# Degree stage of a graph network kernel: a group's tile counts as one product with a 0/1 row selector, turned by way of DRAM, and five slots for the one-hots

## The reference

```python
edge_index = jnp.stack([src, dst])
x = _layernorm(x + _L0_gnn_ref(x, edge_index, edge_weight, W, b))
x = _layernorm(x + _L1_gnn_ref(x, edge_index, edge_weight1, ...))

def _L0_gnn_ref(x, edge_index, edge_weight, W, b):
    row = jnp.concatenate([edge_index[0], loop])
    col = jnp.concatenate([edge_index[1], loop])
    w = jnp.concatenate([edge_weight, jnp.ones((N,))])
    deg = segment_sum(w, row)
    dinv = where(deg > 0, safe ** -0.5, 0)
    norm_w = dinv[row] * w * dinv[col]
    agg = segment_sum(norm_w[:, None] * x[col], row)
    return agg @ W.T + b
```

## Time and profile before

| | us |
|---|---|
| median of three runs | 11022.18 (11020.18 to 11026.79) |
| the profiled execution | 11028.62 |
| its span, first to last instruction | 11026.6 |
| degree stage, its loop over 625 groups | 150.3 to 1149.7 |
| degree stage, what follows to the barrier | 1149.7 to 1225.7 |

### The profile page before, as it was taken

How to read it: one execution, slowest core, us unless ns; L and a number is a source line. 1 busy time by engine, 2 the same in 40 slices (tenths; PEclk the granted TensorE clock), 3 DMA queues, 4 the chain that set the end, 5 groups by cost and what they waited for, 6 DMA issues and landing times. The chain is left out here.

```text
span 11026.6 us, 234377 instructions
## 1 busy us (share of the span) xinstructions
PE 7327.8 (66%) x59805; PEld 5900.2 (54%) x59806; DVE 5508.2 (50%) x18225; ACT 3051.0 (28%) x10603; POOL 6784.5 (62%) x7028
## 2 busy tenths in 40 slices
PE   5999333333333333333566667999999999999999
PEld 4888211111222222222455546888888888888875
DVE  5888533333333333333799965444444444444443
ACT  4888211111111111111577721111111111111111
POOL 0000277777777777777555514777777777777771
PEclk9999655555555555555555555555555555555555
DMA  6600222222222232232344423333333333333331
GB/s 240 254 0 0 53 77 77 78 77 79 76 78 77 76 78 76 76 78 77 95 111 111 112 77 85 88 86 85 86 86 86 85 86 86 86 85 86 86 82 32
DMA packets 627619, 950.47 MB, mean 86 GB/s; under 512 B 202831, under 2 KB 381213, under 8 KB 627329
## 3 DMA queue, kind: packets, MB, share of 16 engines
q1 hardware_dynamic: 427582, 640.84, 20.8%
q0 software_dynamic: 200000, 309.20, 10.0%
HBM read 690.33 MB, written 259.09 MB: 86 GB/s over the span
## 5 line engine op out<-in xcount | busy, mean ns | idle before, releaser
L862 POOL DMA_INDIRECT moved<-tables,place x3125 | 3076.2, 984 | 2079.8 <-ACT tables L853 1134.2
L1260 POOL DMA_INDIRECT tables<-a_half,src_i x3125 | 3070.9, 983 | 1271.7 <-issue 944.5
L824 PE MATMUL ps_rows<-tables,dst_hot 128*128 x10830 | 808.0, 240 | 2633.2 <-ACT tables L853 1495.9
L824 PEld LDWEIGHTS ps_rows<-tables,dst_hot 128*128 128x128 bf16 x10830 | 668.1, 125 | 2977.4 <-issue 2934.4
L852 ACT ACTIVATE tables<-ps_rows,edge_cols 128x64 f32<-128x64 f32 x3125 | 707.3, 318 | 3365.9 <-DMA moved<-tables,place 3225.2
L1381 PE MATMUL ps_msum<-tables,src_cols 128*128 128x64 f32 x6250 | 1497.9, 427 | 0.0
L1381 PEld LDWEIGHTS ps_msum<-tables,src_cols 128*128 128x128 f32 x6250 | 1380.4, 329 | 136.6 <-issue 136.6
L1362 ACT ACTIVATE src_cols<-src_cols 128x640 f32<-128x640 f32 x625 | 460.5, 737 | 3512.9 <-DVE src_cols L1285 3448.9
L1285 DVE TENSOR_TENSOR src_cols<-ps_pre,tables 128x640 f32<-128x640 f32 x625 | 515.0, 824 | 1735.9 <-DMA tables<-a_half,src_i 1732.3
L788 DVE CAST place<-place_f 128x5 int32<-128x5 f32 x625 | 109.6, 175 | 2116.7 <-DMA moved<-tables,place 2112.4
L1408 PE MATMUL ps_pre<-b_rows,tables 64*128 64x128 bf16 x9375 | 1110.0, 309 | 0.0
(11 more groups left out here) (230 smaller groups left out, 9804.3 us busy)
## 6 DMA issues: line engine op xcount, KB each, us to landing
dst_rows<-in_dst SPq DMA_DIRECT2D x625, 320.0 KB
tables<-moved SPq DMA_DIRECT2D x723, 162.5 KB, 2.2
moved<-sums SPq DMA_DIRECT2D x180, 650.0 KB, 7.7
m_dst_rows<-in_dst SPq DMA_DIRECT2D x625, 160.0 KB
moved<-tables,place POOLq DMA_INDIRECT x3125
tables<-a_half,src_i POOLq DMA_INDIRECT x3125
b_rows<-b_half SPq DMA_DIRECT2D x625, 48.0 KB
base_rows<-tile_bases SPq DMA_DIRECT2D x625, 2.9 KB
```

The lines of the kernel that those rows point to most:

```text
L824: last = pe.matmul(ps_rows[:, h, j * D:(j + 1) * D], dst_hot[:, slot, j * P:(j + 1) * P], cols(parts, win * (3 * D) + i * D, D), start=beg ...
L862: pool.indirect_dma_start(out=moved[:, :], out_offset=bass.IndirectOffsetOnAxis(ap=place[:, s, j:j + 1], axis=0), in_=rows[:, s, j, :], in ...
L1260: pool.indirect_dma_start(out=a_rows[:, s, j, :], out_offset=None, in_=a_dram[:, :], in_offset=bass.IndirectOffsetOnAxis(ap=src_i[:, s, j: ...
```

## The change

Counting: the group's whole `hi_hot` (490 columns) is now the moving side of one product (new line 673). The weights are a row selector `select[:, row, :]`, 128 x 25 in bf16, whose column `row` is all ones and the others zero. So the product adds the 490 column sums of the group to row `row` of a 25 x 490 PSUM tile, and 25 groups share one bank. GpSimd makes the selector in two memsets, for which TensorE waits once.

ScalarE empties a bank after each 25th group, as 25 x 490, into one of two halves of `group_counts`, and from the third time on first waits until the DMA that reads that half has landed (`counts_kept[h]`). SyncE stores the half in the DRAM array `tile_counts`; these 25 stores come on SyncE after the zero fill. After the last, one DMA loads the whole array as `by_tile`, with the tile of a block on the partition. The transposes and the copies are gone; VectorE waits for the load (`laid`) before its sums over blocks.

The one-hots have five slots (SC = 5) for S = 4. The bodies of TensorE's and ScalarE's loops have 50 groups for 8, VectorE's 5 for 4. `q_le` moves into the big buffer `sums`.

```diff
-    REST = NG // S * S
+    SC = 5
+    RG = 25
...
-        lo_hot = sb("lo_hot", [P, S, G, P], F32)
-        hi_hot = sb("hi_hot", [P, S, G, NW], BF16)
+        lo_hot = sb("lo_hot", [P, SC, G, P], F32)
+        hi_hot = sb("hi_hot", [P, SC, G, NW], BF16)
+        select = sb("group_rows", [P, RG, RG], BF16)
...
-        ps_tile = ctx.enter_context(nc.psum_tensor("ps_tile_counts", [P, 2, 512], F32))
+        ps_tile = ctx.enter_context(nc.psum_tensor("ps_tile_counts", [RG, 2, 512], F32))
-        by_window = tables[0:NW, 0:2 * TILES].bitcast(F32)
+        group_counts = tables[0:RG, 0:4 * G * NW].bitcast(F32).rearrange("p (a b) -> p a b", a=2)
...
-        q_le = sb("q_le", [P, QP, NW], F32)
+        q_le = sums[:, 1400:1400 + QP * NW].rearrange("p (a b) -> p a b", a=QP)
...
+            def keep(r, h, use):
+                sp.wait_ge(evacuated, r + 1)
+                sp.dma_start(tile_counts[bass.ds(r * (RG * G * NW), RG * G * NW)].rearrange("(p e) -> p e", p=RG),
+                             group_counts[:, h, :]).then_inc(counts_kept[h], 16)
             for i in range(NQ // ZG * ZG, NQ):
                 sp.dma_start(moved[i * GE:(i + 1) * GE, :].rearrange("(p r) c -> p (r c)", p=P),
                              zeros[:, 0:G * ROW]).then_inc(zero_done, 16)
+            over_pairs(sp, NG // RG, keep)
+            sp.wait_ge(counts_kept[0], 16 * ((NG // RG + 1) // 2))
+            sp.wait_ge(counts_kept[1], 16 * (NG // RG // 2))
+            sp.dma_start(by_tile, tile_counts.rearrange("(a p b) -> p a b", p=BT, b=NW)).then_inc(laid, 16)
...
+            rows = select[:, :, :].rearrange("p a b -> p (a b)")
+            pool.memset(rows, 0.0).then_inc(select_made, 1)
+            pool.wait_ge(select_made, 1)
+            pool.memset(rows[:, 0:RG * RG:RG + 1], 1.0).then_inc(select_made, 1)
...
-                wait(dve, used, g - (S - 1))
+                wait(dve, used, g - (SC - 1))
...
-            for r in range(NB // BR):
-                dve.wait_ge(turned, r + 1)
-                then(dve.tensor_copy(by_tile[:, r * BR:(r + 1) * BR, :], split3(ps_turn[0:BT, r % 2, 0:BR * NW], BR)))
-                dve.engine_nop().then_inc(laid, 1)
+            dve.wait_ge(laid, 16)
...
-                if t % S == S - 1:
+                if t % RG == RG - 1:
+                    h = t // RG
                     act.wait_ge(counted, g + 1)
-                    act.activation(cols(by_window, (g - (S - 1)) * G, S * G), ps_tile[0:NW, t // S, 0:S * G], ACT.Copy).then_inc(evacuated, 1)
-            over_groups(act, NG, body, slots=2 * S)
+
+                    wait(act, counts_kept[h], use * 16)
+                    act.activation(group_counts[:, h, :], ps_tile[:, h, 0:G * NW], ACT.Copy).then_inc(evacuated, 1)
+            over_groups(act, NG, body, slots=2 * RG)
...
-                for j in range(G):
-                    last = pe.matmul(ps_tile[0:NW, t // S, s * G + j:s * G + j + 1], hi_hot[:, s, j, :], ones_bf[:, 0:1], start=True, stop=True)
-                last.then_inc(counted, 1)
+                pe.matmul(ps_tile[:, h, 0:G * NW], select[:, row, :], hi_hot[:, s, :, :], start=row == 0, stop=row == RG - 1,
+                          skip_group_check=True).then_inc(counted, 1)
...
-            for r in range(NB // BR):
-
-                wait(pe, laid, r - 1)
-                for a in range(BR):
-                    last = pe.transpose(ps_turn[0:BT, r % 2, a * NW:(a + 1) * NW], by_window[:, (r * BR + a) * BT:(r * BR + a + 1) * BT], ident[0:NW, 0:NW])
-                last.then_inc(turned, 1)
```

More of the change, by code:

```diff
@@ L122, in split3, with program @@
     return ap.rearrange("p (a b) -> p a b", a=n)
-def program(nc, x, src, dst, w, attr, W, b, W1, b1, W2, b2, W_ih, b_ih, W_hh, b_hh, out, places, table, moved, tile_base, a_dram, x1_dram, x1T_dram, attr9, c_dram, b_dram, rel_table, base_dram):
+def program(nc, x, src, dst, w, attr, W, b, W1, b1, W2, b2, W_ih, b_ih, W_hh, b_hh, out, places, table, moved, tile_base, a_dram, x1_dram, x1T_dram, attr9, c_dram, b_dram, rel_table, base_dram, tile_counts):
     with ExitStack() as ctx:
@@ L183, in program @@
         steps_table(nc, dst, before, node_id, table, rel_table, base_dram, sums, step_tab, rel_tab, base_col, base_lane, q_tab)
-        counts(nc, lane_row, ident, ones_bf, ones, before, tables, src_hi, src_lo, weight, moved, places, tile_base, sums, dinv, start_row, q_tab, attr_in_parts)
+        counts(nc, lane_row, ident, ones_bf, ones, before, tables, src_hi, src_lo, weight, moved, places, tile_base, sums, dinv, start_row, q_tab, attr_in_parts, tile_counts)
         scaled_nodes(nc, x, xs, dinv, tables, acc, node_id, base_col, base_lane)
@@ L478, in _, with counts @@
             split_bf16(dve, then, wide[:, 0, :], wide[:, 1, :], [parts[:, i, :] for i in range(3)], attr_done)
-def counts(nc, lane_row, ident, ones_bf, ones, before, tables, src_hi, src_lo, weight, moved, places, tile_base, sums, dinv, start_row, q_tab, attr_in_parts):
+def counts(nc, lane_row, ident, ones_bf, ones, before, tables, src_hi, src_lo, weight, moved, places, tile_base, sums, dinv, start_row, q_tab, attr_in_parts, tile_counts):
     ZG = 4
     BR = 5
-    REST = NG // S * S
+    SC = 5
+    RG = 25
+    assert NG % (2 * RG) == RG and RG % SC == 0
     with ExitStack() as ctx:
@@ L569, in body @@
                                   cols(src_lo, g * G, G).unsqueeze(2).to_broadcast([P, G, P]), ALU.is_equal).then_inc(chain, 1)
-            over_groups(dve, NG, body)
+            over_groups(dve, NG, body, slots=SC)
             n = NG
@@ L629, in weigh @@
                 act.wait_ge(hot_made, g + 1)
-                wait(act, used, g - (S - 1))
+                wait(act, used, g - (SC - 1))
                 for j in range(G):
@@ L649, in _ @@
             pe.wait_ge(pad_cleared, 1)
+            pe.wait_ge(select_made, 2)
             def body(g, t, use, _):
                 first, last_one = is_first(g), isinstance(g, int) and g == NG - 1
-                s = t % S
+                s, h, row = t % SC, t // RG, t % RG
                 pe.wait_ge(hot_made, g + 1)
-                if s == 0:
-                    wait(pe, evacuated, use * 2 + t // S - 1)
-                for j in range(G):
-                    last = pe.matmul(ps_tile[0:NW, t // S, s * G + j:s * G + j + 1], hi_hot[:, s, j, :], ones_bf[:, 0:1], start=True, stop=True)
-                last.then_inc(counted, 1)
+                if row == 0:
+                    wait(pe, evacuated, use * 2 + h - 1)
+                pe.matmul(ps_tile[:, h, 0:G * NW], select[:, row, :], hi_hot[:, s, :, :], start=row == 0, stop=row == RG - 1,
+                          skip_group_check=True).then_inc(counted, 1)
                 pe.wait_ge(weighted, g + 1)
@@ L679, in _ @@
             for r in range(NB // BR):
-                wait(pe, laid if r < 2 else split, NB // BR if r < 2 else r - 1)
+                wait(pe, split, r - 1)
                 pe.matmul(ps_turn[0:BT, r % 2, 0:BR * NW], before[0:BT, 0:BT], by_tile[:, r * BR:(r + 1) * BR, :], start=True, stop=False)
@@ L1639 @@
     base_dram = nc.dram_tensor("group_bases", (NG,), F32, kind="Internal").ap()
-    program(nc, *args, result, q_windows, steps, moved, tile_base, a_dram, x1_dram, x1T_dram, attr9, c_dram, b_dram, rel_table, base_dram)
+    tile_counts = nc.dram_tensor("tile_counts", (TILES * NW,), F32, kind="Internal").ap()
+    program(nc, *args, result, q_windows, steps, moved, tile_base, a_dram, x1_dram, x1T_dram, attr9, c_dram, b_dram, rel_table, base_dram, tile_counts)
     r = run_bass_kernel_spmd(nc, [arrays], core_ids=[0])
```

14 lines of the change are left out of this document (6 added, 8 removed).

## The result

The change makes the kernel slower: 11313.44 us (four runs, 11308.43 to 11316.46) against 11021.18 for the kernel before on the same chip, a ratio of 1.0264, 95% interval 1.0246 to 1.0281. The forecast was 11128 with a range to 11180: the sign and the wait were right, the size was not. The profiled execution took 11312.33, its span is 11310.5, 283.9 longer than before.

The account below looks back on a forecast made before the run. Only the degree stage could move the time, with TensorE, VectorE and ScalarE each about 0.9 busy. Its loop ending 94.7 us later (store wait, pace, code) plus 11 for the tail gave +106 on 11022.2: 11128 us, range 11085 to 11180.

Parts of the forecast that it names:

- The wait at group 74: Degree stage: ScalarE waits for the first store of counts, behind SyncE's zero fill; due about 256 us, standstill some 206 us.
- The landing: First store of counts: issued no earlier than 460.00, small store 2.06 us, so landed at 462.1; late end 478.
- The rival of the late engine: First store lands at 478, behind one DMA engine still busy with zero fill; total 11144 us, chance 0.20.
- the pace: Degree loop's other 550 groups: ScalarE binds at 1.34 us a group, 34.5 us per 25 groups, 759 us for 22 blocks.
- The range of the pace: Degree loop, per block of 25 groups: 34.2 us to 36.3, the latter if VectorE's loop takes 1.42 a group.
- The rival of a slow pace: Degree loop: VectorE at 1.42 us a group or a dearer wide product, 40 us more, total 11168; chance 0.12.
- The code term: ScalarE's 559-row degree loop: code read again at each of 10 jumps back, 2.06 us each, 21 us in all.
- The tail: Last degree product to sums over blocks: store and load of counts replace transposes and copies, costing 11 us more.
- The later stages, put at nothing: Stages after the degree stage: instructions unchanged, so their length was to stay the same, 0 us.
- The rival in which the wait doesn't bind: First store lands before about 256 us; the degree loop ends 114 us earlier, total 10919; chance 0.05.

## Why the prediction was wrong in size

The wait at group 74 was right in place and kind. Group 74 was due at 460.45 - 185.78 = 274.7, not 256, since its 75 groups already ran at 1.62 us. The landing came out by luck: the zero fill ended 15.6 us earlier than in the profile before, and the store took 16.0 us for the 2.06 that I took; the two cancel, 460.4 for 462.1. The rival of the late engine was right in its mechanism. From 451 to 458 the DMA share is 0.06, which is one engine of 16 with what is left of the zero fill, and 0.02 behind it. Of the 50 rows of the first two stores, the records show 40 moved between 448.8 and 450.8, and the last ten one after another from 459.45 to 460.3, behind the last packet of the zero fill at 457.84 (windows of the kernel after: stretch, length, busy and count by engine, granted clock, DMA share, GB/s):

```profile
445.00:460.00 15.00, 0.00 (x0) 0.00 (x0) 0.00 (x0) 0.00 (x0) 0.00 (x0) 0.50 0.26 97
451.00:458.00 7.00, 0.00 (x0) 0.00 (x0) 0.00 (x0) 0.00 (x0) 0.00 (x0) 0.50 0.06 25
461.00:470.00 9.00, 7.60 (x33) 6.03 (x33) 2.83 (x5) 9.00 (x36) 0.00 (x0) 0.58 0.02 6
```

The step that failed is the pace: "TensorE then needs 1.12 + 0.20 = 1.32, or up to 1.35 if changing weights costs as now". The product's 0.20 was right, as the wide selector shows (0.21). The mistake was the price of changing weights, taken from the 98-column counts as at most 0.03; it is 0.30 a group with 25 columns. A bank takes 40.95 for 34.5, 6.45 x 22 = 142 us. The range of the pace, 34.2 to 36.3 a bank, varied only ScalarE, VectorE and a switch "as now", so the term had no bound for the new shape. The rival of a slow pace named a dearer wide product and was priced at 40 us: right in its direction, but neither the product nor VectorE was the cause, and TensorE became the bound where ScalarE had been expected to be. The profile before had a row that warned: in messages, products with one column as the weights stand ahead of products with 128, and the load of the latter idles 136.6 us over 625 steps for "issue", the same row that stands after (L1388 above): 136.6 / 625 = 0.22 us a switch. That is at a granted clock of 0.50 and for one side of the switch alone, and that the width is its cause was not tested there. Taken as it is it would have given 0.22 x 550 = 121 of the 142 us. I read only rows of the same stage for it.

The code term was right in kind and half in size: ten jumps, at 44.4 us in all over the 40.95 of their banks (3.9 to 5.6 each, for 2.06), with 68 more reads for the 40 forecast. Beside the reads it costs the clock. TensorE idles 2.77 us for ScalarE there, and then the granted clock is down for some us. The same view, just ahead of a jump and behind it:

```profile
500.00:504.00 4.00, 4.00 (x29) 3.06 (x27) 3.35 (x5) 0.00 (x0) 0.00 (x0) 1.00 0.00 0
508.00:511.50 3.50, 2.96 (x15) 2.32 (x16) 1.23 (x2) 3.50 (x14) 0.00 (x0) 0.72 0.00 0
```

Of the Trainium skill, "Runtime: NRT & Kernel Launch", section "Instruction fetch mechanics", gives these engines room for 512 instructions, in blocks of 16 KiB, and TensorE 2048. The rule that a jump out of the room stalls agrees with the runs. Its sizes don't fit ScalarE here: a body of some 280 rows is read again, and the reads are of 0.73 MB / 89 = 8 KB. For TensorE the runs agree: its bodies of 48 and 50 groups are read once, 26 reads, of 0.43 MB / 26 = 16 KB.

The tail was 8.6 for 11: the load was issued at 1410.84 and landed by 1426.4, 15.6 for 17.5; VectorE's wait was 13.50 for 17 to 20. The later stages, put at nothing, took 15 more, and that is open. Together, against the forecast: pace +142, jumps +23, later stages +15, tail -2, the wait's end -2, and +3 for the cold clock behind it: +179, for a span 178 longer than 11026.6 + 106.

The rival in which the wait doesn't bind was put at 10919: with the store freed, the selector wide and the loops nested it is 10913.28 on a chip where the kernel before takes 26 less, so that rival's 103 us of gain came out as 82. That is nearer than it deserves. In the profiled executions on one chip the loop ends 133.4 us earlier (1147.18 to 1013.78) for the rival's 114, which still had 21 for code; the tail takes 9.1 more for 11; and the later stages, put at nothing, take back 50.9.

## What to carry to other kernels

Where a change brings in a shape, price the switch to and from its neighbours, not only the instruction, and look through all stages for a row with such a neighbour. The idle for "issue" ahead of a weight load is a lower bound of that price: after the change it is 356.9 - 232.1 = 124.8 us over 625 groups, 0.20 a group of the 0.30. Where a narrow selector stands among wide weights, a wide one that slides over zeros can be the cheaper. A loop that is unrolled to match a buffer's period has to fit the engine's code room; a nested loop keeps the period and the room. And a small store put behind a long row of big DMAs is as late as the slowest engine that works on them.

## What the runs showed of the hardware that I had not expected

- A product with 25 or 64 columns of weights between products with 128 costs 0.30 us more a group than one with 128, at full clock: the weights behind it load 0.31 us after its own, not 0.12, and its own load begins with its product, not 0.11 us ahead. Weights of 98 columns are loaded 0.11 us ahead; their price behind was not measured.
- A ScalarE loop of about 280 rows or more is read again at each jump, in reads of 8 KB, at 3.9 to 5.6 us a jump with what the clock adds. Beside a running zero fill it is 6.4 to 7.0 us for the body of 559 rows and 11 for that of 280, where reads begin 4.9 us apart for 2.1. A nest of some 130 rows on ScalarE is not read again, nor one of 194 on VectorE, nor TensorE's of 50 groups.
- A DMA of 25 rows issued right behind 183 big ones landed 16 us after its issue, since its last rows stood behind the slowest engine's rest of the fill; on GpSimd's queue such stores landed after 5.0 to 8.2 us beside the fill and 1.8 behind it, and held nobody up.
